# The last feed-forward stage's low-rank product, written as two column tiles of token halves

## What is computed

```
P = jnp.einsum('bsd,dr->bsr', x, U1)                        # 256 channels -> rank 64
H = jax.nn.gelu(jnp.einsum('bsr,rf->bsf', P, V1) + b1)      # rank 64 -> 1024
Q = jnp.einsum('bsf,fr->bsr', H, U2)                        # 1024 -> rank 64
return jnp.einsum('bsr,rd->bsd', Q, V2) + b2                # rank 64 -> 256
...
x = x + jnp.tanh(g_ffn[1]) * _L1_ffn_ref(_layernorm(x, axis=-1), ...)
```

## Time and profile before

| | |
|---|---|
| median of 3 runs | 769.09 us (767.45 to 769.4) |
| the profiled execution's own time | 770.5 us |
| its span, first to last instruction | 768.7 us |
| TensorE / DVE / ScalarE busy | 91% / 67% / 54% of the span |
| mean granted TensorE clock | 0.963 of 2.4 GHz |
| stage d's eight bodies | about 663 us to the end |

### The profile page before, as it was taken

The page is one execution under the profiler, slowest core; times in us unless marked ns, Lnnn a source line. Parts: engine busy times, 40 slices in busy tenths (PEclk is TensorE's granted clock), DMA queues, the critical chain, the costliest instruction groups (busy, mean ns, idle before and its releaser), DMA issues.

```text
span 768.7 us, 12459 instructions
## 1 busy us (share of the span) xinstructions
PE 703.1 (91%) x3826; PEld 491.1 (64%) x3826; DVE 518.5 (67%) x998; ACT 418.9 (54%) x1127; POOL 206.4 (27%) x278
## 2 busy tenths in 40 slices
PE   3788999999999996699999999999999986799996
PEld 1465655554544365588888888888888865456554
DVE  7576477666675376778887877788878787423423
ACT  1666655535545531565566566655665565345352
POOL 3555433310110031533322323233223220212120
PEclk9679999999999998799999999999999999899999
DMA  6621203810000022333334444333344330001112
GB/s 196 219 84 55 83 29 104 234 55 1 0 1 1 0 48 63 83 92 97 82 90 110 110 110 110 81 81 81 86 110 110 82 83 1 1 1 55 35 48 82
DMA packets 46021, 57.48 MB, mean 75 GB/s; under 512 B 14080, under 2 KB 24480, under 8 KB 45856
## 3 DMA queue, kind: packets, MB, share of 16 engines
q1 hardware_dynamic: 45984, 57.03, 27.4%
HBM read 27.52 MB, written 4.19 MB: 41 GB/s over the span
## 4 chain that ended last, share of the span: by engine, by line
PE 77%; ACT 9%; DVE 9%; issue 3%; POOL 0%; DMA 0%; DVEq 0%; ACTq 0%
PE bank L1037 11%; PE bank L1219 7%; ACT c_p L859 7%; PE bank L1292 7%; PE bank L1271 6%; PE bank L1049 5%; PE bank L1411 4%; PE bank L1285 4%; PE bank L1013 4%; PE bank L1258 4%; PE bank L1237 3%; PE bank L1017 3%; DVE c_nmx L1709 3%; PE bank L1402 2%; PE bank L1323 2%
## 5 line engine op out<-in xcount | busy, mean ns | idle before, releaser
L859 ACT ACTIVATE c_p<-bank,c_nmx 128x256 f32<-128x256 f32 x256 | 117.5, 487 | 42.9 <-DVE c_nmx L1709 42.9
L1722 DVE TENSOR_TENSOR c_p<-c_p,c_inv 128x1024 f32<-128x1024 f32 x64 | 91.6, 1432 | 1.1
L1037 PE MATMUL bank<-b_o,cw 128*128 128x512 f32 x192 | 90.8, 603 | 0.0
L1709 DVE TENSOR_REDUCE c_nmx<-bank 128x4 f32<-128x1024 f32 x64 | 75.3, 1219 | 19.9 <-PE bank L1258 19.9
L1271 PE MATMUL bank<-ident,c_p 128*128 128x128 f32 x512 | 65.2, 276 | 8.2 <-ACT c_p L859 8.2
L1271 PEld LDWEIGHTS bank<-ident,c_p 128*128 128x128 f32 x512 | 58.5, 143 | 16.0 <-ACT c_p L859 8.9
L945 ACT ACTIVATE d_h<-bank,b_col 128x512 f32<-128x512 f32 x64 | 39.6, 686 | 45.8 <-PE bank L1403 45.7
L1219 PE MATMUL bank<-c_ctxT,wsrcT 128*128 128x256 f32 x256 | 62.0, 387 | 1.4 <-ACT c_ctxT L835 1.4
L728 ACT ACTIVATE b_h<-bank,cb 128x512 f32<-128x512 f32 x48 | 33.0, 687 | 53.8 <-PE bank L1037 53.7
L1037 PEld LDWEIGHTS bank<-b_o,cw 128*128 128x128 f32 x192 | 34.2, 190 | 41.6 <-issue 41.2
L1729 DVE COPY c_pT<-bank 128x512 f32<-128x512 f32 x64 | 43.9, 686 | 23.8 <-PE bank L1271 23.8
(11 more groups left out here) (185 smaller groups left out, 1450.5 us busy)
## 6 DMA issues: line engine op xcount, KB each, us to landing
c_stack<-c_parts SPq DMA_DIRECT2D x192, 128.0 KB
a_ctx<-in_ctx SPq DMA_DIRECT2D x16, 512.0 KB, 3.4
c_ctx<-in_ctx SPq DMA_DIRECT2D x16, 512.0 KB, 3.5
out_x<-x_sb SPq DMA_DIRECT2D x8, 512.0 KB, 3.0
x_sb<-in_x SPq DMA_DIRECT2D x3, 1024.0 KB, 7.5
mask_b<-in_mask_BxS_fk SPq DMA_DIRECT2D x1, 2048.0 KB, 11.7
x_sb<-in_x SPq DMA_DIRECT2D x2, 512.0 KB, 7.4
wsrc_raw<-in_L_xattn_W_src SPq DMA_DIRECT2D x1, 1024.0 KB, 7.1
```

Source lines behind the costliest of these rows:

```text
L859: op = nc.scalar.activation(c_p[hg][:, tc, j, :], scores(tc)[:, j, :], ACT.Exp, bias=c_nmx[hg][:, tc, j:j + 1], accum_out=c_sum[hg][:, tc, ...
L1037: op = mm(bank[2 * u + h][:], cw1[:, c, h * P:(h + 1) * P], b_o[n % LANES][:, c, :], start=c == 0, stop=c == DK - 1)
L1709: v.tensor_reduce(c_nmx[hg][:, tc, :], scores(tc), AXIS.X, ALU.max, negate=True)\
L1722: v.tensor_tensor(pr, pr, c_inv[hg][:, :, js].unsqueeze(3).to_broadcast([P, TS, 2, S]), ALU.mult)\
```

## The change

`u1_sb` holds U1 once. The low-rank product is made of four matmuls with 64 weight columns and 256 tokens each in place of two with 128 columns and 512 tokens: the first 256 tokens go to rows 0 to 63 of bank 4, the other 256 to rows 64 to 127, both in columns 0 to 255. On DVE the high parts of each half are written to the rows where the product stands, and the low parts to the opposite rows: for tokens 0 to 255 high above and low below as before, for tokens 256 to 511 the reverse. Since V1 stands twice, the hidden product doesn't change. Each of DVE's two instructions becomes two, of 64x256. One load of U1 (64 KB) goes, and the buffers behind `u1_sb` move by 512 bytes.

```
-        u1_sb = sb("u1_sb", [P, DK, 2 * RANK])
+        u1_sb = sb("u1_sb", [P, DK, RANK])
...
-            (u1_sb[:, :, 0:RANK], u1.rearrange("(c p) r -> p c r", p=P)),
-            (u1_sb[:, :, RANK:2 * RANK], u1.rearrange("(c p) r -> p c r", p=P)),
+            (u1_sb[:], u1.rearrange("(c p) r -> p c r", p=P)),
...
                 for c in range(DK):
-                    op = mm(bank[4][:], u1_sb[:, c, :], d_xnT[s][:, c, :], start=c == 0, stop=c == DK - 1)
+                    for half in range(2):
+                        op = mm(bank[4][half * RANK:(half + 1) * RANK, 0:HALF], u1_sb[:, c, :],
+                                d_xnT[s][:, c, half * HALF:(half + 1) * HALF], start=c == 0, stop=c == DK - 1)
                 op.then_inc(d_p_ps, 1)
...
-                v.tensor_copy(d_pT[s][:], bank[4][:]).then_inc(d_phi, 1)
+                parts = [slice(half * RANK, (half + 1) * RANK) for half in range(2)]
+                tokens = [slice(half * HALF, (half + 1) * HALF) for half in range(2)]
+                for half in range(2):
+                    op = v.tensor_copy(d_pT[s][parts[half], tokens[half]], bank[4][parts[half], 0:HALF])
+                op.then_inc(d_phi, 1)
                 need(dve, d_phi, n + 1)
-                low = slice(RANK, 2 * RANK)
-                v.tensor_tensor(d_pT[s][low, :], bank[4][low, :], d_pT[s][low, :].bitcast(F32),
-                                ALU.subtract).then_inc(d_p_ok, 1)
+                for half in range(2):
+                    op = v.tensor_tensor(d_pT[s][parts[1 - half], tokens[half]], bank[4][parts[half], 0:HALF],
+                                         d_pT[s][parts[half], tokens[half]].bitcast(F32), ALU.subtract)
+                op.then_inc(d_p_ok, 1)
```

## The result

The changed kernel takes 763.67 us (median of 16 runs, 758.11 to 766.43) against 768.53 us (16 runs, 763.77 to 770.36) for the kernel before: ratio 0.9933, 95% interval 0.9916 to 0.9951, which is 3.8 to 6.5 us and about 5.1 in the middle. The forecast was 5.2. Three of the changed kernel's sixteen executions and one of the other's are some 5 us shorter than the rest, which widens the interval and lifts its middle. Without these four the medians are 764.30 and 768.72, 4.4 us apart. (Those 5 us arise in the first 100 us of the kernel, far ahead of the change, as "The two kernels once more" shows.)

The account below looks back on a forecast made before the run. TensorE's queue bounds stage d, with DVE on the path's edge. Gains 0.45 + 0.84 + 3.20 + 0.70 = 5.19 us took the profiled 770.5 to 765.3, and the 769.09 median to 763.9 us; range 762.3 to 766.3.

Parts of the forecast that it names:

- The product: Low-rank product on TensorE: starts 0.10 later, hands over in 1.01; 1.11 in place of 1.81 us, 0.70 gained per ordinary body.
- rival 3: Low-rank product: tiles don't run side by side, about 1.97 us in place of 1.81; 770.9 us; included in a 0.09 chance.
- DVE's four instructions: Low-rank operands on DVE: two roundings and two subtractions of 64x256 take 1.60 us, 0.15 more than before.
- rival 1: DVE's four instructions don't overlap, taking 1.82 us; gain 3.9, time 765.2 us; chance 0.20 together with milder clock mixtures.
- two instructions with no wait between overlap by 0.08: DVE's roundings and subtractions: each pair overlaps by 0.08 us, as pairs L1729 and L1693 do in the trace.
- My estimate of 1.70: DVE's four instructions unoverlapped at the skill's 424 ns each: 1.70 us, gain some 0.6 us less; set aside for the trace.
- How the two meet: Ordinary body of stage d: L1827 has 0.09 us slack, becomes 0.06 late and delays the transposes; gain 0.64 of 0.70.
- Bodies 1 to 5 are like this: Stage d's looped bodies: all five gain the same 0.64 us as the body read, 3.20 in all.
- Stage c: Its last body: TensorE's 0.60 us gain less DVE's 0.15, whose instructions stand in the chain releasing L1285; 0.45 gained.
- Body 0: First body of stage d: L1827 already waits 0.47 for TensorE, so DVE's 0.15 hides; gain 0.84 us.
- Rival 2: DVE's 64x256 instructions cost 0.69 us like 64x512 ones: 3.5 us slower, 772.6; most of a 0.04 chance.
- Rival 4: Clock's low stretch at 663 to 679 us may shift; half a body longer gives a gain of about 3, 766.

Follow-up runs that it names:

- The two kernels once more: Both kernels run and profiled again unchanged: the kernel before 767.96 us (ratio 0.9995), the changed kernel 763.55 us.
- one-tile version: Changed kernel with both halves in rows 0 to 63 of the bank, one behind the other, and two DVE instructions of 64x512: 769.22 us, ratio 1.0017.
- DVE on the same rows: Product in one column tile, with DVE's four 64x256 instructions all reading rows 0 to 63: 765.1 us in one execution, one of the short ones.

## Why the prediction was right

**The product**: forecast 0.10 later to start and 1.01 to hand over, measured 0.09 and 1.02. The one-tile version shows that it is the two tiles side by side, so rival 3 is out. (Its price of 1.97 isn't what its terms give, 8 x 0.21 + 2 x 0.10 = 1.88; that 0.10 + 1.87 came out for the one-tile version is chance.) The Trainium skill's drain on a change of tiling mode (TensorEngine Tiling (Array Packing), Key Properties) stands in the same 0.10; it is there with one tile as well.

**DVE's four instructions** were mis-sized: forecast 1.60, measured 1.79, close to the upper bound (given as 1.82; 4 x 0.45 is 1.80) and so to rival 1's price. The step that failed is "two instructions with no wait between overlap by 0.08": the pairs I took it from stay on the same rows, these change from rows 0 to 63 to rows 64 to 127, and don't overlap. Rival 1's reason, that the writes go to other rows than they come from, is not it ("DVE on the same rows"). My estimate of 1.70 from the Trainium skill's float32 figure (VectorE: DVE Perf Modes, the section on TRN2's extra fixed latency) was nearer to the truth than my sum: 424 ns by the figure, 422 measured. It was still 0.09 short, of which 0.07 are the two gaps that the estimate leaves out. The Trainium skill's advice on short instructions in that section is given for data read from SBUF; the roundings here read PSUM, so these runs don't test it.

**How the two meet.** I had L1834 end 1.41 behind its start before L1827 could begin, 0.09 of slack. In the changed kernel L1840 stands at 732.49 and L1833 at 733.81, 1.32 apart: when DVE isn't waiting, the copy too starts ahead of its predecessor's end. So the slack was 0.18. The two errors, 0.19 too little for the operands and 0.09 too little slack, partly cancel by luck: L1833 is 0.28 behind TensorE and not the 0.17 forecast. The five ordinary bodies gave 2.83 for 3.20. That "what is late next is L1742, and behind it the whole body" held in bodies 2, 4 and 5. "Bodies 1 to 5 are like this" did not: the body that the forecast read was the one without a wait. In bodies 1 and 3 of the kernel before, L1742 started 0.45 and 0.63 behind the copy and not 0.34, and TensorE already waited for it; there the new lateness cost nearly nothing. Rival 1 had the price and not the effect: it counted the same short slack and came to 3.9 in all, against 4.5.

**Stage c**: 0.60 - 0.15 became 0.60 - 0.34, 0.25 measured. With DVE at two instructions the part gained 0.55. In the changed kernel TensorE now stands idle ahead of the last update product, where the earlier trace rows have no idle time:

```profile
656.06 1.07 PE L1284 MATMUL bank<-c_pT,c_v 128*32 128x256 f32 x16 [0.28 <-issue]
```

With two DVE instructions that idle time is gone. The chain was the right one.

**Body 0**: 0.77 for 0.84. I said that the 0.15 would hide, since L1827 waited 0.47, and priced the cover of the hidden product only in an ordinary body (1.2 us). Body 0 has no output product behind L1323, and there the operands come last. TensorE in body 0 of the changed kernel:

```profile
674.51 1.90 PE L1412 MATMUL bank<-d_h,u_sb 128*64 128x256 f32 x16
676.53 0.50 PE L1403 MATMUL bank<-d_pT,v_hi 128*128 128x512 f32 x1
```

and DVE:

```profile
675.62 0.86 DVE L1757 TENSOR_TENSOR d_pT<-bank,d_pT 64x256 fp32r<-64x256 f32 x2
```

TensorE hands over 2.02 us behind the start of L1412, where 1.88 is its own pace; L1757 ends at 676.48, 0.05 ahead. So 0.14 us were lost to a wait that the prediction took as covered, and 0.05 because the eight records hand over after 0.92 and not 0.87. Some 0.11 came back: the transposes of this part no longer wait (0.29 to 0.23) and then hand over in 0.97 in place of 1.02.

**Rival 2** would have needed 0.61 us for each DVE instruction; they take 0.42 each. **Rival 4**, the clock, was right that the low stretch may differ and silent on the sign; in the profiled execution that stretch was worth 1.4 us on top of the change, and whether the change had a part in it isn't shown. Taken with the 1.5 us ahead of all changed instructions, it is why the difference of two spans, 7.3 us, would have been a poor measure here.

The time came out at 763.67 for 763.9, and that it is so close is partly luck. By parts the change was worth 4.5 us and not 5.2, nearly all of the shortfall on DVE. The forecast started from 769.09, the median of three executions, where sixteen have 768.53; that start, 0.56 too high, hid most of the gain's being 0.7 too high. The lower end of the range, 762.3, is also 0.4 below what its terms give (769.1 - 5.4 - 1 = 762.7).

## What to carry to other kernels

Two products with 64 output rows each over half the tokens take about the time of one (1.02 us for both here, 1.87 one behind the other) when their outputs lie in different halves of the rows; the gain can be read beforehand from any product of the kernel that already does so. Then ask who unpacks the result: halves in different rows turn two full instructions into four short ones on another engine, and where that engine shares the path, even at 40% busy, it takes part of the gain back (in stage c 0.34 of 0.60 us). Look at each place of the path by itself, the first and the last body above all, since the work that covers a chain in the loop may be missing there; and don't price a loop from one body, since others may already have a wait at the same place.

## What was not expected of the hardware

- Two DVE instructions in a row overlap by 0.09 us when they stay on the same rows (0.75 for two of 0.42) and not at all when the second goes from rows 0 to 63 to rows 64 to 127 (0.86).
- With nothing to wait for, DVE's copy starts 1.32 us behind a pair of additions that is 1.41 long.
- Transposes that start behind a wait hand TensorE over after 1.02 us, others after 0.97.
- Behind the last layer norm the lower clock level lasted 3.4 or 6.8 us, with one and the same kernel in one case, and in one version it fell into stage c instead.
